# Product-key retrieval with 136 candidate sums of a head in place of 256

## The chip, the cores and the metric

One NeuronCore of a Trainium2 chip runs the whole program; the other cores are idle. The metric is the device time of one execution in microseconds (us), as the median of several executions. All times inside the kernel come from one profiled execution and count from the start of its span.

## What is computed

The program chains eight sublayers over 128 tokens of width 512: four graph layers and four feed-forward layers. The change lies in the fourth, a retrieval by product keys. Of its reference this matters:

```python
q = x @ w_q * (1.0 / np.sqrt(1.0 + BN_EPS))
queries = q.reshape(b, n, 2, HEADS, DIM_KEY).transpose(2, 0, 1, 3, 4)
sim = jnp.einsum('pbnhd,hkpd->pbnhk', queries, keys)
v0, i0 = jax.lax.top_k(sim[0], TOPK)
all_scores = v0[..., :, None] + i0[..., None, :].astype(v0.dtype)
all_scores = all_scores.reshape(*all_scores.shape[:-2], -1)
scores, pk_indices = jax.lax.top_k(all_scores, TOPK)
h = jnp.einsum('bnd,bnhkd->bnhk', q, weights_down)
h = jax.nn.gelu(h)
h = h * jax.nn.softmax(scores, axis=-1)
out = jnp.einsum('bnhk,bnhkd->bnd', h, weights_up)
```

There are 8 heads, 256 keys and a TOPK of 16. The second summand is an index, not a value, so each token and head has 16 best values (sorted, largest first) and their 16 indices; all 16 x 16 sums of a value and an index are formed, the best 16 of these 256 are picked, and their places 0 to 255 name the rows of two tables, `weights_down` and `weights_up`.

A sum of row i (the i-th best value) and the index of rank j among the 16 indices has at least (i + 1)(j + 1) - 1 sums that are no smaller. In rows 8 to 15 an entry whose index is not the largest has at least 17 such sums, so only the entry of the largest index can be among the best 16 there. That leaves 8 x 16 + 8 = 136 candidates.

## The kernel before

All tokens lie on the 128 partitions. Each engine has a queue of its own that is written out by hand in program order; an engine stops at the first wait that isn't met, and waits are on semaphores that other engines (or itself) raise. The retrieval runs from about 104 to 137 us of the span.

**VectorE** runs `search_and_pick(n, n - 2)` (from line 2337) for n = 0 to 9, ten passes. A pass searches head n (n < 8): the 8 largest of its 256 similarities (line 2344), a replacement of these by a very small number (2352), their indices (2357), the next 8 (2359) and their indices (2366). Between these stand the four steps of picking for head p = n - 2 among its 256 sums: the best 8 (2348), their replacement (2355), the next 8 (2362), and a replacement that leaves the rest (2371). At even p from 2 on comes a reciprocal of two heads' weight sums (2375). Head 7's weights are made by VectorE itself (2380), and after the last pass the last reciprocal (2387) and one diagonal (2390).

**ScalarE** (lines 962 to 1002) first computes the GELU (959) and loads the table of the exponential (961). Then for each n in this order: the negated best sum of head n - 2 (964) and the exponentials of its sums (966), the sum of head n - 3's weights (976), the exponentials of head n - 2's rest (971), and the cast of head n's indices to floats (981).

**POOL** (lines 724 to 753) has, for each n: the 256 sums of head n (728, once its cast is done), the weights of head n - 2 (737: exponentials of all sums less those of the rest, so that only the picked keep a weight), and for even n from 4 on two diagonals (745), matrices with the reciprocals of a head's weight sum on the diagonal.

**TensorE** multiplies a head's 128 x 256 weights by its diagonal and adds up the heads (1573), two 128-column halves per head. In between stand parts of later sublayers and spare matmuls against the identity (1220). After the last head the sums are scaled on VectorE (2395) and go through the second table (1581) into the residual.

Four buffers rotate over the heads for the sums, exponentials, rest and weights. The weight matrix of a head always has all 256 columns, since a column stands for a row of the tables.

Of the kernel before, what the change touches and what calls it, by code (L numbers as in the profile page):

```python
# [26 lines left out]
P = 128  # L27
D = 512
CH = D // P
H = 8  # L30
# [19 lines left out]
PICKS = TOPK * TOPK  # L50

# [136 lines left out]
def build(nc, A, out):  # L188
# [14 lines left out]
    with ctx:  # L203
# [112 lines left out]
        best = sb("best", [P, 4, TOPK])  # L316
        negbest = sb("negbest", [P, 4])
# [55 lines left out]
        kv_sb = prob_store[:, :].rearrange("p (b n) -> p b n", b=4)  # L373
        peer_all, peer_exp, peer_rest, peer_pick = (
# [306 lines left out]
        def _(pool):  # L681
# [19 lines left out]
            pool.tensor_scalar(gat_cap[:], ident[:], -2.0 * GAT_NEG, GAT_NEG, ALU.mult, ALU.add).then_inc(sig("gat_loops_ready"), 1)  # L701
# [22 lines left out]
            def head_sums(h):  # L724
                pool.wait_ge(*at("peer_index_ready", h + 1))
                if h:
                    pool.wait_ge(*at("peer_sum_ready", h))
                pool.tensor_tensor(peer_all[:, h % 4, :].rearrange("p (i j) -> p i j", i=TOPK),
                                   topv[:, h % 4, :].unsqueeze(2).broadcast_to([P, TOPK, TOPK]),
                                   topif[:, h % 4, :].unsqueeze(1).broadcast_to([P, TOPK, TOPK]), ALU.add) \  # L730
                    .then_inc(sig("peer_sum_ready"), 1)

            def picked_weights(p):
# [3 lines left out]
                pool.tensor_tensor(peer_pick[:, p % 4, :], peer_exp[:, p % 4, :], peer_rest[:, p % 4, :], ALU.subtract) \  # L737
# [96 lines left out]
        def _(act):  # L834
# [127 lines left out]
            def exp_of_sums(h):  # L962
# [3 lines left out]
                nc.scalar.activation(peer_exp[:, h % 4, :], peer_all[:, h % 4, :], ACT.Exp,  # L966
                                     bias=negbest[:, h % 4:h % 4 + 1]).then_inc(sig("peer_exp_ready"), 1)

            def exp_of_rest(p):
                act.wait_ge(*at("peer_pick_step", PICK_STEPS * (p + 1)))  # L970
                nc.scalar.activation(peer_rest[:, p % 4, :], peer_rest[:, p % 4, :], ACT.Exp,
                                     bias=negbest[:, p % 4:p % 4 + 1]).then_inc(sig("peer_rest_ready"), 1)

            def sum_of_weights(p):
                act.wait_ge(*at("peer_picked", p + 1))
# [1051 lines left out]
        def _(dve):  # L2027
# [130 lines left out]
            dve.wait_ge(*at("gat_loops_ready", 1))  # L2158
# [178 lines left out]
            def search_and_pick(h, p):  # L2337
# [7 lines left out]
                q, work2 = p % 4, peer_work2[:, p % 2, :]  # L2345
                if pick:
                    dve.wait_ge(*at("peer_sum_ready", p + 1))
                    dve.max(best[:, q, 0:8], peer_all[:, q, :]).then_inc(sig("peer_pick_step"), 1)
# [4 lines left out]
                if pick:  # L2353
                    picked(p, 1)
                    dve.match_replace(work2, best[:, q, 0:8], peer_all[:, q, :], NEG).then_inc(sig("peer_pick_step"), 1)
# [11 lines left out]
                if pick:  # L2367
                    picked(p, 3)
                    if p >= 4:
                        dve.wait_ge(*at("peer_picked", p - 3))  # L2370
# [519 lines left out]
```

## Time and profile before

| what | value |
|---|---|
| median of 3 runs | 435.19 us (435.03 to 435.54) |
| the profiled execution | 435.27 us |
| its span, first to last instruction | 433.6 us |
| mean granted TensorE clock | 0.988 of full speed |
| busy in the span: TensorE, VectorE, ScalarE, POOL | 401.1, 197.3, 128.7, 47.2 us |

The profile is of one execution. The page gives busy times, a chain of waits followed back from the last instruction, and the costliest groups of instructions; the timelines give single instructions with their start and listed duration. A listed duration runs from start to end of one instruction, and neighbours on one engine can overlap, so starts and durations say different things. Of two identical instructions the distance of their starts is what the engine spends.

### The profile page before, as it was taken

What the parts mean: (1) busy time and instruction counts of PE and PEld (TensorE: products, weight loads), DVE (VectorE), ACT (ScalarE), POOL (GpSimd) and SP (SyncE); (2) the same over time, 40 slices, a digit from 0 to 9 for tenths busy, and PEclk for the clock granted to TensorE, in tenths of its full rate; (3) what the DMA queues carried; (4) which work ended last, traced back from release to release, by engine and by line L of the source; (5) the groups of instructions that cost most, each with busy time, mean ns of one, the idle gap of its engine ahead of it and who ended that gap; (6) DMA issues with size and microseconds to landing.
All of it is one profiled execution on the core that took longest, in us unless ns stands there. A gap on an engine that the chain in (4) does not pass through costs nothing.

```text
span 433.6 us, 7726 instructions
## 1 busy us (share of the span) xinstructions
PE 401.1 (93%) x2854; PEld 295.0 (68%) x2854; DVE 197.3 (45%) x575; ACT 128.7 (30%) x381; POOL 47.2 (11%) x101
## 2 busy tenths in 40 slices
PE   7998999896588989999999998998999999999996
PEld 6698665796077869997455655665688994493482
DVE  4844545555995244401324558687733531201102
ACT  2313312514453102332300564462113232122130
POOL 4000010010364000011002122011100000000000
PEclk9999999999689999999999999999999999999999
DMA  8999359449002000899998555851920599999900
GB/s 287 383 427 353 122 203 411 163 191 389 3 2 70 29 0 26 310 392 299 374 334 323 182 166 130 303 183 62 400 98 2 226 423 421 421 419 421 384 2 24
DMA packets 19721, 101.44 MB, mean 234 GB/s; under 512 B 3639, under 2 KB 5559, under 8 KB 8804
## 3 DMA queue, kind: packets, MB, share of 16 engines
q1 hardware_dynamic: 19396, 100.94, 61.0%
q8 instruction: 22, 0.36, 0.3%
q14 instruction: 15, 0.12, 0.1%
q10 hardware_dynamic: 288, 0.02, 0.0%
HBM read 100.68 MB, written 0.26 MB: 233 GB/s over the span
## 4 chain that ended last, share of the span: by engine, by line
PE 72%; DVE 12%; issue 7%; ACT 3%; POOL 3%; DVEq 2%; POOLq 0%; ACTq 0%
PE ps L1251 13%; PE ps L1237 12%; PE ps L1636 7%; PE ps L1919 6%; PE ps L1664 4%; PE ps L1220 3%; PE ps L1730 2%; PE ps L1398 2%; PE ps L1653 2%; PE ps L1228 1%; PE ps L1726 1%; PE ps L1985 1%; PE ps L1435 1%; PE ps L1350 1%; PE ps L1271 1%
## 5 line engine op out<-in xcount | busy, mean ns | idle before, releaser
L1220 PE MATMUL ps<-ident 128*128 128x128 f32 x350 | 48.5, 291 | 2.8 <-POOL ident L690 2.8
L1220 PEld LDWEIGHTS ps<-ident 128*128 128x128 f32 x350 | 45.5, 204 | 5.3 <-POOL ident L690 2.8
L1251 PEld LDWEIGHTS ps<-y_t,ew 128*128 128x128 f32 x352 | 39.9, 192 | 1.7 <-issue 1.7
L1251 PE MATMUL ps<-y_t,ew 128*128 128x128 f32 x352 | 40.2, 275 | 0.0
L1636 PE MATMUL ps<-y_t,ew 128*128 128x128 f32 x256 | 29.2, 276 | 0.0
L1636 PEld LDWEIGHTS ps<-y_t,ew 128*128 128x128 f32 x256 | 28.8, 192 | 0.0
L2449 DVE COPY dense<-ps 128x512 f32<-128x512 f32 x8 | 5.5, 692 | 43.7 <-PE ps L1237 43.7
L1237 PE MATMUL ps<-ew,y_t 128*128 128x512 f32 x56 | 25.1, 596 | 0.0
L2731 DVE SCALAR_TENSOR_TENSOR t<-prob_store 128x512 f32<-128x512 f32 x6 | 4.2, 692 | 36.4 <-ACT prob_store L1154 20.4
L867 ACT ACTIVATE prob_store<-ps,nmax_s 128x128 f32<-128x128 f32 x48 | 16.9, 381 | 10.6 <-DVE nmax_s L2111 10.5
L1237 PEld LDWEIGHTS ps<-ew,y_t 128*128 128x128 f32 x56 | 10.2, 190 | 12.0 <-issue 11.8
L1029 ACT ACTIVATE dense<-ps,bqk 128x128 f32<-128x128 f32 x32 | 9.1, 369 | 19.9 <-PE ps L1636 19.9
L855 ACT COPY x<-ps 128x256 f32<-128x256 f32 x10 | 3.7, 372 | 30.3 <-DVE part_st L2075 18.2
L1553 PE MATMUL ps<-dense,eq_t 128*8 128x512 f32 x8 | 5.9, 912 | 7.3 <-ACT big L966 7.3
L1251 PE MATMUL ps<-y_t,dense 128*128 128x128 f32 x96 | 11.2, 277 | 0.7 <-ACT y_t L847 0.7
L1251 PEld LDWEIGHTS ps<-y_t,dense 128*128 128x128 f32 x96 | 10.9, 192 | 1.1 <-issue 1.1
L1237 PE MATMUL ps<-dense,y_t 128*128 128x512 f32 x24 | 11.2, 601 | 0.0
L1237 PE MATMUL ps<-ew,x_t 128*128 128x512 f32 x24 | 11.1, 597 | 0.0
L1884 PE MATMUL ps<-ew,z_t 128*128 128x256 f32 x48 | 10.9, 381 | 0.1
L1664 PE MATMUL ps<-ew,z_t 128*32 128x512 f32 (+1 forms) x56 | 10.9, 597 | 0.0
L705 POOL TENSOR_TENSOR ln_rstd<-ln_mv,minus_half 128x1 f32<-128x1 f32 x8 | 4.6, 570 | 56.6 <-DVE ln_mv L2077 31.2
L774 POOL TENSOR_TENSOR ln_rstd<-ln_mv,minus_half 128x1 f32<-128x1 f32 x10 | 5.5, 545 | 47.9 <-DVE ln_mv L2463 47.9
(545 smaller groups left out, 755.7 us busy)
## 6 DMA issues: line engine op xcount, KB each, us to landing
ew<-in_l_w SPq DMA_DIRECT2D x20, 1024.0 KB, 21.4
dense<-in_l_w SPq DMA_DIRECT2D x12, 1024.0 KB, 20.8
ew<-in_l_wk SPq DMA_DIRECT2D x8, 1024.0 KB, 9.7
ew<-in_l_wq SPq DMA_DIRECT2D x7, 1024.0 KB, 6.1
ew<-in_l_wv SPq DMA_DIRECT2D x6, 1024.0 KB, 8.9
ew<-in_l_wo SPq DMA_DIRECT2D x5, 1024.0 KB, 4.9
ew<-in_gqa_wq SPq DMA_DIRECT2D x3, 1024.0 KB, 10.8
ew<-in_gqa_wk SPq DMA_DIRECT2D x3, 1024.0 KB, 15.4
```

The lines of the kernel that those rows point to most:

```text
L867: last = nc.scalar.activation(prob[:, s, :], ps[:, 3 + a, g * P:(g + 1) * P], ACT.Exp, bias=nmax_s[:, s:s + 1], scale=scale, accum_out=rsu ...
L1029: last = nc.scalar.activation(k_all[:, e, c * P:(c + 1) * P], ps[:, 1 + e % 2, c * P:(c + 1) * P], ACT.Identity, bias=bqk[:, e * 12 + CH + ...
L1220: pe.matmul(ps[:, b, 3 * P:4 * P], ident[:], ident[:], start=True, stop=True)
L1237: return pe.matmul(bank(b), in_t[:, c, :], w[:, c, :], start=(c == 0), stop=(c == CH - 1))
L1251: last = pe.matmul(ps[:, b, m * n:(m + 1) * n], w[:, c, (first + m) * P:(first + m + 1) * P], in_t[:, c, 0:n], start=(c == 0), stop=(c == ...
L1398: last = pe.matmul(ps[:, b, m * P:(m + 1) * P], w[:, m, c, :], y_t[:, c, :], start=(c == 0), stop=(c == CH - 1))
L1636: last = pe.matmul(ps[:, 1 + e % 2, m * P:(m + 1) * P], l2_w("k", e)[:, c, m * P:(m + 1) * P], y_t[:, c, :], start=(c == 0), stop=(c == CH ...
L1653: last = pe.matmul(ps[:, 0, m * P:(m + 1) * P], l2_w("q", p)[:, c, m * P:(m + 1) * P], y_t[:, c, :], start=(c == 0), stop=(c == CH - 1))
L1664: last = pe.matmul(ps[first:end, b, 0:columns.stop - columns.start], in_t[:, c, first:end], l2_w(kind, L2_STEPS[t][a])[:, c, columns], sta ...
L1730: last = pe.matmul(ps[:, b, 0:D // 2], ctx_t[:, c, :], l2_w("o", L2_STEPS[t][0])[:, c, columns], start=(c == 0), stop=(c == CH - 1))
L1884: last = pe.matmul(ps[:, b, 0:D // 2], z_t[:, c, :], l2_w("gcn", k)[:, c, half * D // 2:(half + 1) * D // 2], start=False, stop=(c == CH - 1))
L1919: last = pe.matmul(ps[cols_of, b, :], in_t[:, c, cols_of], w_of[:, c, :], start=(c == 0 and not started), stop=(c == CH - 1))
```

## The change

VectorE takes the largest of a head's 16 indices (`top_index`) and a mark of where it lies (`top_hot`); both stand in the pass after the head's search. POOL forms 8 x 16 sums and 8 further ones, of values 8 to 15 with the largest index. The four picking steps and the two exponentials work on 136 elements. The weights of the 8 late candidates are computed as a column of 8 (`pick_rest`) and spread over 8 x 16 columns by a product with the mark, so that the weight matrix again has 256 columns. Head 7's weights are made in two parts on VectorE, with a drain behind each. POOL's sums now wait for the largest index rather than for the cast, and for no earlier sum. A semaphore used once at the start is replaced by a further step of another.

```diff
@@ -48,6 +48,9 @@
 KEYS = 256
 TOPK = 16
 PICKS = TOPK * TOPK
+ROWS = TOPK // 2
+FULL = ROWS * TOPK
+CANDIDATES = FULL + TOPK - ROWS
 
 SEARCH_STEPS = 5
 PICK_STEPS = 4
@@ -314,6 +317,10 @@
         topi = sb("topi", [P, 4, TOPK], U32)
         topif = sb("topif", [P, 4, TOPK])
         best = sb("best", [P, 4, TOPK])
+        top_index = sb("top_index", [P, 4])
+        top_hot = sb("top_hot", [P, 4, TOPK])
+        pick_rest = sb("pick_rest", [P, 4, TOPK - ROWS])
+        rest_sum = sb("rest_sum", [P, 2])
         negbest = sb("negbest", [P, 4])
         picksum = sb("picksum", [P, H])
         pickinv = sb("pickinv", [P, H])
@@ -371,6 +378,11 @@
         peer_work, peer_work2 = (tile[:, :].rearrange("p (b n) -> p b n", b=2) for tile in (t1, h2))
         wide = big[:, :].rearrange("p (a n) -> p a n", a=2)
         kv_sb = prob_store[:, :].rearrange("p (b n) -> p b n", b=4)
+        def rows_by_top(q, tile, hot):
+            return (tile.rearrange("p (i j) -> p i j", i=ROWS),
+                    pick_rest[:, q, :].unsqueeze(2).broadcast_to([P, TOPK - ROWS, TOPK]),
+                    hot.unsqueeze(1).broadcast_to([P, TOPK - ROWS, TOPK]))
+
         peer_all, peer_exp, peer_rest, peer_pick = (
             tile.rearrange("p (b n) -> p b n", b=4) for tile in (
                 big[:, 0:4 * PICKS], big[:, 4 * PICKS:8 * PICKS], prob_t[:].rearrange("p h n -> p (h n)"),
@@ -698,7 +710,7 @@
                                    fill=1.0, base=0, pattern=[[-1, H], [0, P]], channel_multiplier=1) \
                     .then_inc(sig("gat_r_ready"), 1)
             pool.wait_ge(*at("gat_r_ready", 2))
-            pool.tensor_scalar(gat_cap[:], ident[:], -2.0 * GAT_NEG, GAT_NEG, ALU.mult, ALU.add).then_inc(sig("gat_loops_ready"), 1)
+            pool.tensor_scalar(gat_cap[:], ident[:], -2.0 * GAT_NEG, GAT_NEG, ALU.mult, ALU.add).then_inc(sig("const_ready"), 1)
 
             def layer_norm_rstd(k):
                 pool.wait_ge(*at("ln_var_ready", k + 1))
@@ -722,19 +734,26 @@
             batch_norm_rstd(1)
             layer_norm_rstd(3)
             def head_sums(h):
-                pool.wait_ge(*at("peer_index_ready", h + 1))
-                if h:
-                    pool.wait_ge(*at("peer_sum_ready", h))
-                pool.tensor_tensor(peer_all[:, h % 4, :].rearrange("p (i j) -> p i j", i=TOPK),
-                                   topv[:, h % 4, :].unsqueeze(2).broadcast_to([P, TOPK, TOPK]),
-                                   topif[:, h % 4, :].unsqueeze(1).broadcast_to([P, TOPK, TOPK]), ALU.add) \
+                pool.wait_ge(*at("peer_top_step", 2 * h + 1))
+                pool.tensor_tensor(peer_all[:, h % 4, 0:FULL].rearrange("p (i j) -> p i j", i=ROWS),
+                                   topv[:, h % 4, 0:ROWS].unsqueeze(2).broadcast_to([P, ROWS, TOPK]),
+                                   topif[:, h % 4, :].unsqueeze(1).broadcast_to([P, ROWS, TOPK]), ALU.add) \
+                    .then_inc(sig("peer_sum_ready"), 1)
+                pool.tensor_tensor(peer_all[:, h % 4, FULL:CANDIDATES], topv[:, h % 4, ROWS:TOPK],
+                                   top_index[:, h % 4:h % 4 + 1].broadcast_to([P, TOPK - ROWS]), ALU.add) \
                     .then_inc(sig("peer_sum_ready"), 1)
 
             def picked_weights(p):
                 pool.wait_ge(*at("peer_rest_ready", p + 1))
                 if p >= 4:
                     pool.wait_ge(*at("peer_head_added", p - 3))
-                pool.tensor_tensor(peer_pick[:, p % 4, :], peer_exp[:, p % 4, :], peer_rest[:, p % 4, :], ALU.subtract) \
+                pool.tensor_tensor(pick_rest[:, p % 4, :], peer_exp[:, p % 4, FULL:CANDIDATES],
+                                   peer_rest[:, p % 4, FULL:CANDIDATES], ALU.subtract).then_inc(sig("peer_picked"), 1)
+                pool.tensor_tensor(peer_pick[:, p % 4, 0:FULL], peer_exp[:, p % 4, 0:FULL], peer_rest[:, p % 4, 0:FULL],
+                                   ALU.subtract).then_inc(sig("peer_picked"), 1)
+                pool.wait_ge(*at("peer_picked", 3 * p + 1))
+                pool.wait_ge(*at("peer_top_step", 2 * p + 2))
+                pool.tensor_tensor(*rows_by_top(p % 4, peer_pick[:, p % 4, FULL:], top_hot[:, p % 4, :]), ALU.mult) \
                     .then_inc(sig("peer_picked"), 1)
 
             def diagonals(k):
@@ -963,16 +982,16 @@
                 act.wait_ge(*at("peer_pick_step", PICK_STEPS * h + 1))
                 nc.scalar.mul(negbest[:, h % 4:h % 4 + 1], best[:, h % 4, 0:1], -1.0).then_inc(sig("peer_negbest_ready"), 1)
                 act.wait_ge(*at("peer_negbest_ready", h + 1))
-                nc.scalar.activation(peer_exp[:, h % 4, :], peer_all[:, h % 4, :], ACT.Exp,
+                nc.scalar.activation(peer_exp[:, h % 4, 0:CANDIDATES], peer_all[:, h % 4, 0:CANDIDATES], ACT.Exp,
                                      bias=negbest[:, h % 4:h % 4 + 1]).then_inc(sig("peer_exp_ready"), 1)
 
             def exp_of_rest(p):
                 act.wait_ge(*at("peer_pick_step", PICK_STEPS * (p + 1)))
-                nc.scalar.activation(peer_rest[:, p % 4, :], peer_rest[:, p % 4, :], ACT.Exp,
+                nc.scalar.activation(peer_rest[:, p % 4, 0:CANDIDATES], peer_rest[:, p % 4, 0:CANDIDATES], ACT.Exp,
                                      bias=negbest[:, p % 4:p % 4 + 1]).then_inc(sig("peer_rest_ready"), 1)
 
             def sum_of_weights(p):
-                act.wait_ge(*at("peer_picked", p + 1))
+                act.wait_ge(*at("peer_picked", 3 * (p + 1)))
                 nc.scalar.activation(peer_exp[:, p % 4, :], peer_pick[:, p % 4, :], ACT.Identity,
                                      accum_out=picksum[:, p:p + 1]).then_inc(sig("peer_weights_summed"), 1)
 
@@ -2155,7 +2174,7 @@
                     .then_inc(sig("gat_r_scaled"), 1)
 
             dve.wait_ge(*at("edges_counted", 1))
-            dve.wait_ge(*at("gat_loops_ready", 1))
+            dve.wait_ge(*at("const_ready", 4))
             dve.scalar_tensor_tensor(gat_cap[:], ps[:, 5, 0:P], -2.0 * GAT_NEG, gat_cap[:], ALU.mult, ALU.add) \
                 .then_inc(sig("gat_capped"), 1)
             settle()
@@ -2342,17 +2361,28 @@
                     sim, work = ps[:, 1 + h // 2, w * KEYS:(w + 1) * KEYS], peer_work[:, w, :]
                     dve.wait_ge(*at("peer_sim_ready", h // 2 + 1))
                     dve.max(topv[:, b, 0:8], sim).then_inc(sig("peer_search_step"), 1)
-                q, work2 = p % 4, peer_work2[:, p % 2, :]
+                q, work2 = p % 4, peer_work2[:, p % 2, 0:CANDIDATES]
                 if pick:
-                    dve.wait_ge(*at("peer_sum_ready", p + 1))
-                    dve.max(best[:, q, 0:8], peer_all[:, q, :]).then_inc(sig("peer_pick_step"), 1)
+                    dve.wait_ge(*at("peer_sum_ready", 2 * (p + 1)))
+                    dve.max(best[:, q, 0:8], peer_all[:, q, 0:CANDIDATES]).then_inc(sig("peer_pick_step"), 1)
+                r = h - 1
+                if 0 <= r < H:
+                    dve.wait_ge(*at("peer_index_ready", r + 1))
+                    dve.tensor_reduce(top_index[:, r % 4:r % 4 + 1], topif[:, r % 4, :], AX.X, ALU.max) \
+                        .then_inc(sig("peer_top_step"), 1)
 
                 if search:
                     searched(h, 1)
                     dve.match_replace(work, topv[:, b, 0:8], sim, NEG).then_inc(sig("peer_search_step"), 1)
                 if pick:
                     picked(p, 1)
-                    dve.match_replace(work2, best[:, q, 0:8], peer_all[:, q, :], NEG).then_inc(sig("peer_pick_step"), 1)
+                    dve.match_replace(work2, best[:, q, 0:8], peer_all[:, q, 0:CANDIDATES], NEG).then_inc(sig("peer_pick_step"), 1)
+                if 0 <= r < H:
+                    dve.wait_ge(*at("peer_top_step", 2 * r + 1))
+                    if r >= 4:
+                        dve.wait_ge(*at("peer_picked", 3 * (r - 3)))
+                    dve.tensor_scalar(top_hot[:, r % 4, :], topif[:, r % 4, :], top_index[:, r % 4:r % 4 + 1], None, ALU.is_equal) \
+                        .then_inc(sig("peer_top_step"), 1)
                 if search:
                     dve.max_index(topi[:, b, 0:8], topv[:, b, 0:8], sim).then_inc(sig("peer_search_step"), 1)
                     searched(h, 2)
@@ -2367,8 +2397,8 @@
                 if pick:
                     picked(p, 3)
                     if p >= 4:
-                        dve.wait_ge(*at("peer_picked", p - 3))
-                    dve.match_replace(peer_rest[:, q, :], best[:, q, 8:16], work2, NEG).then_inc(sig("peer_pick_step"), 1)
+                        dve.wait_ge(*at("peer_picked", 3 * (p - 3)))
+                    dve.match_replace(peer_rest[:, q, 0:CANDIDATES], best[:, q, 8:16], work2, NEG).then_inc(sig("peer_pick_step"), 1)
 
                 if p >= 2 and p % 2 == 0:
                     dve.wait_ge(*at("peer_weights_summed", p))
@@ -2377,8 +2407,14 @@
                     picked(p, 4)
                     dve.wait_ge(*at("peer_exp_ready", H))
                     dve.wait_ge(*at("peer_head_added", H - 4))
-                    dve.scalar_tensor_tensor(peer_pick[:, q, :], peer_rest[:, q, :], NEG, peer_exp[:, q, :], ALU.is_equal,
-                                             ALU.mult, accum_out=picksum[:, p:p + 1]).then_inc(sig("peer_pick_step"), 1)
+                    for part, out in ((slice(FULL, CANDIDATES), pick_rest[:, q, :]), (slice(0, FULL), peer_pick[:, q, 0:FULL])):
+                        k = 0 if part.start else 1
+                        dve.scalar_tensor_tensor(out, peer_rest[:, q, part], NEG, peer_exp[:, q, part], ALU.is_equal,
+                                                 ALU.mult, accum_out=rest_sum[:, k:k + 1])
+                        settle()
+                    dve.tensor_tensor(picksum[:, p:p + 1], rest_sum[:, 0:1], rest_sum[:, 1:2], ALU.add)
+                    dve.tensor_tensor(*rows_by_top(q, peer_pick[:, q, FULL:], top_hot[:, q, :]), ALU.mult) \
+                        .then_inc(sig("peer_pick_step"), 1)
 
             for n in range(H + PICK_LAG):
                 search_and_pick(n, n - PICK_LAG)
```

## Rows read from the trace of the kernel before

**Rows 1.** The page's first part: busy time, share of the span and instructions of each engine.

```profile
PE 401.1 (93%) x2854; PEld 295.0 (68%) x2854; DVE 197.3 (45%) x575; ACT 128.7 (30%) x381; POOL 47.2 (11%) x101
```

**Rows 2.** Stretch (us), length, busy (x count) PE, PEld, DVE, ACT, POOL; granted clock, DMA share, GB/s.

```profile
124.00:128.00 4.00, 4.00 (x23) 4.00 (x23) 4.00 (x19) 1.91 (x7) 2.47 (x4) 0.58 0.01 2
128.00:132.00 4.00, 3.44 (x27) 3.15 (x26) 3.07 (x12) 2.95 (x10) 2.25 (x4) 1.00 0.00 0
```

**Rows 3.** The chain of waits, 98 to 150 us: start us, us, what held the chain.

```profile
131.78 0.59 POOL x_t L745
...
132.42 1.29 PE ps L1573 x8
...
140.59 7.38 PE ps L1251 x64
```

**Rows 4.** Timeline of VectorE, one pass: start us, us, engine line operation out<-in.

```profile
114.65 0.42 DVE L2344 MAX8 topv<-ps 128x8 f32<-128x256 f32 x1
114.99 0.41 DVE L2348 MAX8 best<-big 128x8 f32<-128x256 f32 x1
...
117.94 0.15 DVE L2375 RECIPROCAL pickinv<-picksum 128x2 f32<-128x2 f32 x1
```

**Rows 5.** Groups of VectorE by line and shape: busy us, mean ns of one, idle before.

```profile
L2348 DVE MAX8 best<-big 128x8 f32<-128x256 f32 x8 | 3.3, 409 | 0.0
...
L2432 DVE MAX8 gtop<-gate 128x8 f32<-128x8 f32 x2 | 0.3, 170 | 0.1
```

**Rows 6.** Timeline of VectorE, small instructions of a later sublayer.

```profile
170.14 0.23 DVE L2575 TENSOR_SCALAR big<-iota_f,gidxf 128x8 f32<-128x8 f32 x1
170.28 0.23 DVE L2576 TENSOR_SCALAR big<-iota_f,gidxf 128x8 f32<-128x8 f32 x1
...
177.56 0.16 DVE L2558 TENSOR_REDUCE big<-big 128x1 f32<-128x8 f32 x1
177.64 0.15 DVE L2559 TENSOR_REDUCE big<-big 128x1 f32<-128x8 f32 x1
```

**Rows 7.** Timeline of ScalarE at the start of the retrieval.

```profile
106.17 1.28 ACT L961 ACT_TABLE_LOAD   x1
107.47 0.20 ACT L981 CAST topif<-topi 128x16 f32<-128x16 uint32 x1
```

**Rows 8.** Timeline of VectorE, the instruction behind pass 1's first maximum.

```profile
106.33 0.09 DVE L2352 MATCH_VALUE_LOAD t<-topv,ps 128x8 f32 x1
```

**Rows 9.** Timeline of ScalarE, the pass that starts at 114.65 us.

```profile
114.77 0.51 ACT L971 ACTIVATE prob_t<-prob_t,negbest 128x256 f32<-128x256 f32 x1 [0.77 <-DVE prob_t L2371]
115.18 0.19 ACT L981 CAST topif<-topi 128x16 f32<-128x16 uint32 x1
```

**Rows 10.** Groups of ScalarE: an exponential of 128 elements.

```profile
L885 ACT ACTIVATE prob_store<-prob_store,nmax 128x128 f32<-128x128 f32 x8 | 3.1, 390 | 3.1 <-DVE nmax L2170 3.1
```

**Rows 11.** Groups of POOL by line and shape.

```profile
L774 POOL TENSOR_TENSOR ln_rstd<-ln_mv,minus_half 128x1 f32<-128x1 f32 x10 | 5.5, 545 | 47.9 <-DVE ln_mv L2463 47.9
L737 POOL TENSOR_TENSOR prob_store<-big,prob_t 128x256 f32<-128x256 f32 x7 | 5.1, 726 | 1.0 <-ACT prob_t L971 1.0
L728 POOL TENSOR_TENSOR big<-topv,topif 128x256 f32<-128x256 f32 x8 | 4.9, 618 | 21.5 <-ACT topif L981 21.3
...
L770 POOL TENSOR_TENSOR erows<-erows,y 128x512 f32<-128x512 f32 x2 | 2.5, 1270 | 21.8 <-DMA erows<-in_l_rows 21.8
...
L763 POOL MEMSET big<- 128x1 f32 x8 | 0.5, 100 | 0.0
```

**Rows 12.** Timeline of POOL, head 7's sums and head 5's weights.

```profile
128.73 0.62 POOL L728 TENSOR_TENSOR big<-topv,topif 128x256 f32<-128x256 f32 x1 [0.89 <-ACT topif L981]
129.31 0.73 POOL L737 TENSOR_TENSOR prob_store<-big,prob_t 128x256 f32<-128x256 f32 x1
```

**Rows 13.** Timeline of VectorE, head 7's weights and the last reciprocal.

```profile
132.65 0.42 DVE L2380 SCALAR_TENSOR_TENSOR prob_store<-prob_t,big 128x256 f32<-128x256 f32 x1
...
133.12 0.17 DVE L2387 RECIPROCAL pickinv<-picksum 128x2 f32<-128x2 f32 x1
```

## The prediction

> **What bounds the kernel now.** I read four views in this order. The page's first part comes first: TensorE is busy for 93% of the span, VectorE for 45% [rows 1]. An average says little of a stage of 35 us, so the busy time by stretch comes next, over the retrieval: there the reader sees VectorE busy for all 4.00 us of a 4 us stretch, TensorE held up by spare matmuls at a low granted clock, and POOL and ScalarE near half [rows 2]. So between 104 and 128 us VectorE sets the pace. The chain of waits then shows that the last stretch is another one: it leaves VectorE and runs over POOL's diagonal at 131.78 us into the head matmuls at 132.42 us, and from 140.59 us it is TensorE again [rows 3]. What moves those matmuls moves everything after them, one for one: the transfers' share is 0.01 and 0.00 there [rows 2], so no load runs through this end of the stage that could keep its old time. The timelines give the prices.
>
> The profiled execution took 435.27 us (span 433.6 us and 1.67 us around it), 0.08 us over the median of 435.19 us. I add the shift to the median. A measurement of this kernel can tell about 0.2%, 0.87 us, from no change.
>
> I call the ten turns of the VectorE loop passes 0 to 9. Pass n searches head n and picks for head n-2; passes 2 to 7 do both, 8 and 9 only pick.
>
> **The picks, shorter.** Four instructions per head (two maxima, two replacements) fall from 256 to 136 elements. A MAX8 takes 0.409 us on 256 elements and 0.170 on 8 [rows 5], so 0.96 ns an element, and 120 elements fewer save 0.12 us each, 0.48 a head. Instructions without a wait overlap: one MAX8 starts 0.34 us after the one before, though each is listed at 0.41 to 0.42 [rows 4].
>
> **Two small instructions per head, added on VectorE.** The maximum of the 16 indices: the nearest rows are two reductions of 8 elements, 0.08 us from start to start [rows 6]; I take 0.085. The mark (is_equal against a column): two such comparisons start 0.14 us apart [rows 6]; I take 0.145. Together 0.23. So a pass that does both, with no wait, gets 0.48 - 0.23 = 0.25 shorter; six of them: -1.5 us.
>
> Here a rule speaks against the change. By the Trainium skill (VectorE: DVE Perf Modes, The DRAIN you can't avoid) the next instruction cannot issue until the pipe has emptied, so that the count of instructions is what to keep low. By that rule each added instruction would cost its listed time; the starts in the rows show that here it does not. The result it would give is a rival below.
>
> **The wait in pass 1, the largest single term.** The reduction of head 0 stands in pass 1, behind the first maximum of head 1, and waits for ScalarE's cast of head 0's indices. On ScalarE that cast stands behind the loading of the exponential's table, 106.17 to 107.45 us, and ends at 107.47 + 0.20 = 107.67 [rows 7]. Before, only POOL waited for it. VectorE would be at its next instruction at 106.33 us [rows 8]. Now it waits until about 107.71, reduces for 0.085 and goes on at 107.79: +1.46; with the mark 0.145, +1.6 us. Queued behind that wait are all the searches, and nothing covers it, since ScalarE's order is unchanged.
>
> **The same wait in passes 3 to 7.** In the pass that starts at 114.65 us [rows 4], ScalarE's second exponential begins at 114.77, and the cast at 115.18 ends at 115.37 [rows 9], 0.72 into the pass. With 136 elements the exponential falls from 0.51 to about 0.40 (a 128-element one takes 0.390 [rows 10]), so the cast is done at 0.61 and seen at 0.65. VectorE is at the reduction after two maxima, 0.34 + 0.21 = 0.55. The wait is 0.1, and 0.03 in the two passes that come 0.08 later behind a reciprocal: 0.4 in all. Bounds: nothing, if ScalarE is quicker, and 0.2 a pass, if its exponential shrinks by less. Pass 8 then starts at 1.6 - 1.5 + 0.4 = +0.5 us.
>
> **POOL, five instructions where there were two.** Sums of 128, sums of 8, a difference of 8, one of 128, and the spreading product of 128. Nothing shows POOL on two inputs of 8 or 128 elements. Between the listed 0.726 us at 256 elements and 1.270 at 512 [rows 11] lie 2.1 ns an element and 0.18 fixed: 0.45 for a difference of 128, 0.20 for one of 8. The sums, 0.618 at 256 and both inputs spread out, give 0.40 with the same fixed part; the product has their form, 0.40. Bounds for 8 elements: 0.10, a fill of one column, and 0.545, a power of one column, both POOL [rows 11]. For 128 elements: 0.31, half of the sums, and 0.59, a diagonal of 128 columns [rows 3]. I take the two-input line, as nearest in kind. Neighbours overlap by about 0.04 (128.73 to 129.31 us against 0.62 [rows 12]).
>
> **The tail.** From pass 8 on nothing searches, and the path is a relay: ScalarE's exponential of head 5, the cast of head 7, POOL's sums of head 7, its weights of head 5, ScalarE's sum of head 5, its exponential of head 6 (queued behind that sum), POOL's weights of head 6, the diagonal, the matmuls. Changes along it: two exponentials -0.10 each; between cast and sums the reduction steps in, +0.18 (0.16 and two hand-overs, less the one that was); sums 0.36 + 0.16 against 0.58: -0.06; weights 0.16 + 0.41 + 0.40 against 0.71, twice: +0.26 each. Sum +0.44.
>
> VectorE's own end has more to do: the last pass saves 0.48, but head 7's weights, 0.47 us from 132.65 to 133.12 [rows 13], become two masked products with a drain behind each, an addition and a spreading product: about 0.24 + 0.37 + 0.08 + 0.31 = 1.0, +0.53. With the later reciprocal of pass 8 (+0.28) and +0.5 that route ends at +0.8, less than POOL's, so it hides behind it.
>
> At nothing: the renamed semaphore at the start (the same wait, the same event) and the waits for marks of four heads earlier, done a pass before.
>
> **Sum.** +0.5 at pass 8 and +0.44 in the tail: +0.9 us, 435.19 + 0.9 = 436.1 us. By bounds alone: with POOL at its cheap ends (three steps of 8 at -0.1, five of 128 at -0.1) and no waits in passes 3 to 7, POOL's route gives 0.9 - 0.8 - 0.4 = -0.3, and VectorE's, which then sets the end, +0.8 - 0.4 and about 0.4 less for its share of POOL's steps, 0. At POOL's dear ends it is over +3: three steps by 0.34 and five by 0.15 to 0.2, on the path alone, are +1.9, and the loop below adds to it.
>
> **The rivals.** *POOL becomes the bound.* From reduction to reduction there is a loop: POOL's five (1.5), ScalarE's sum (0.5), exponential (0.3), cast (0.2), the reduction and the hand-overs (0.3): 2.8 us. A pass is 3.29 us now (114.65 to 117.94 [rows 4]) and would be 3.1. When POOL's five pass 1.8 us, that loop sets the pass. With the small ones at 0.38, in the middle of their bounds, the pass is 3.2, so some 0.3 over five passes, and the tail gets 0.55 longer: 436.1 + 0.9 = 437.0; at 0.545 it is about 439. For it: fixed costs on POOL are the least known term, and a power of one column costs 0.545. Against: that is a power, and plain differences follow the line. Chance 0.22, around 437.4.
>
> *No change that can be told.* POOL's short instructions lie near the cheap ends and the waits of passes 3 to 7 vanish. The gain of the six passes then pays for pass 1: 435.2 to 435.6. For it: POOL fills a column in 0.10 us. It decides where three short steps cost under 0.4 together. Chance 0.24.
>
> *Faster.* The wait of pass 1 would have to be gone: 436.1 - 1.5 = 434.6. It needs a cast of head 0 before 106.3 us, which the order on ScalarE denies. Chance 0.05.
>
> *Every added instruction costs its listed time.* On VectorE that is 0.16 + 0.23 in place of 0.23, six times: +1.0 on the forecast, 437.1. The overlapping starts speak against it. This is the outcome by the rule named above. Chance 0.05.
>
> *The granted clock.* TensorE's granted clock was 0.58 from 124 to 128 us and 1.00 from 128 to 132 [rows 2]. Were the lower level (1.2 GHz) to hold over the matmuls after 132 us, their 1.29 us for two heads [rows 3] and the like would double: +3, 439. Their order and distances hardly change. Chance 0.03.
>
> **How the numbers follow.** The forecast itself (+0.6 to +1.4) has 0.41. Two thirds of it lie over +0.87, so slower has 0.28 + 0.22 + 0.05 + 0.03 = 0.58; faster 0.05; within 0.2% the rest, 0.37. The range takes in the unmeasurable case down to 435.0 and POOL's middle bounds up to 437.9; outside are the faster case, the dear end of POOL and the clock.
>
> **What would show it.** VectorE idle about 1.4 us near 106.3, released by ScalarE's cast; passes of about 3.1 us; pass 8 starting near 128.4 us; POOL's weights as three rows of about 0.2, 0.45 and 0.40; the matmuls of heads 4 and 5 near 133.3 us; everything after shifted by the same. I am wrong in the mechanism if pass 1 has no such wait, and in size if POOL's 8-element rows are far from 0.2.

## The result, and the profile after

The changed kernel took 437.19 us (median of six executions, 436.42 to 437.22) against 435.26 us for the kernel before on the same chip (six, 435.03 to 435.68): ratio 1.0040, 95% interval 1.0030 to 1.0051 (a ratio is taken over all executions, so it can differ a little from that of the medians). In a second session (e5 below) it took 436.48 against 435.29: 1.0028, 1.0019 to 1.0037. So it is slower, by 1.2 to 1.9 us; the forecast was +0.9, and both results lie inside its range. The profiled execution took 437.22 us, span 435.4. One execution of all that follow, of e6, took 1031.87 us and is left out as a slow run.

The first reading is the page's first part, after:

```profile
PE 403.3 (93%) x2854; PEld 297.2 (68%) x2854; DVE 195.7 (45%) x595; ACT 127.1 (29%) x381; POOL 48.5 (11%) x123
```

Against [rows 1] VectorE has 20 instructions more and is busy 1.6 us less. The shorter picks are there, and the kernel is slower all the same. So the next view is VectorE's timeline, first of the kernel before, at the points that the stage can be measured from (its first search, passes 2 and 8, the first statistics of the residual behind it, and an instruction at 261 us that comes up later):

```profile
103.75 0.43 DVE L2344 MAX8 topv<-ps 128x8 f32<-128x256 f32 x1 [2.42 <-PE ps L1538]
...
108.01 0.41 DVE L2344 MAX8 topv<-ps 128x8 f32<-128x256 f32 x1
...
127.94 0.41 DVE L2348 MAX8 best<-big 128x8 f32<-128x256 f32 x1
...
137.11 0.86 DVE L2075 BATCH_NORM_STATS2 half_st<-ps 128x6 f32<-128x256 f32 x2 [1.46 <-PE ps L1581]
...
261.06 0.88 DVE L2499 SCALAR_TENSOR_TENSOR x<-x,ln_rstd,erows 128x256 f32<-128x256 f32 x2 [0.45 <-issue]
```

The same view of the changed kernel (start us, us, engine, line, operation, output and inputs; in brackets the idle time before it and what ended it):

```profile
103.28 0.43 DVE L2363 MAX8 topv<-ps 128x8 f32<-128x256 f32 x1 [2.42 <-PE ps L1557]
...
107.24 0.17 DVE L2371 TENSOR_REDUCE top_index<-topif 128x1 f32<-128x16 f32 x1 [1.40 <-ACT topif L1000]
107.32 0.08 DVE L2376 MATCH_VALUE_LOAD t<-topv,ps 128x8 f32 x1
...
109.12 0.41 DVE L2363 MAX8 topv<-ps 128x8 f32<-128x256 f32 x1
...
115.27 0.42 DVE L2363 MAX8 topv<-ps 128x8 f32<-128x256 f32 x1
115.61 0.28 DVE L2367 MAX8 best<-big 128x8 f32<-128x136 f32 x1
115.92 0.17 DVE L2371 TENSOR_REDUCE top_index<-topif 128x1 f32<-128x16 f32 x1
116.01 0.08 DVE L2376 MATCH_VALUE_LOAD t<-topv,ps 128x8 f32 x1
...
116.67 0.24 DVE L2384 TENSOR_SCALAR top_hot<-topif,top_index 128x16 f32<-128x16 f32 x1
116.83 0.08 DVE L2387 MATCH_VALUE_LOAD topi<-topv,ps 128x8 f32 x1
...
118.42 0.15 DVE L2405 RECIPROCAL pickinv<-picksum 128x2 f32<-128x2 f32 x1
...
127.88 0.29 DVE L2367 MAX8 best<-big 128x8 f32<-128x136 f32 x1
...
132.38 0.17 DVE L2412 SCALAR_TENSOR_TENSOR pick_rest<-prob_t,big 128x8 f32<-128x8 f32 x1
...
133.41 0.17 DVE L2423 RECIPROCAL pickinv<-picksum 128x2 f32<-128x2 f32 x1
...
137.56 0.86 DVE L2094 BATCH_NORM_STATS2 half_st<-ps 128x6 f32<-128x256 f32 x2 [1.46 <-PE ps L1600]
```

This execution was 0.47 us earlier before anything that the change touches (103.28 against 103.75), so shifts inside the stage are counted from the first search. The whole retrieval, from first search to first statistics, took 137.11 - 103.75 = 33.36 us before and 137.56 - 103.28 = 34.28 after: **+0.92**, against +0.94 by the steps of the prediction (0.5 and 0.44).

The loss is in pass 1. Its reduction waits 1.40 us for ScalarE, whose cast stands behind the table load in the changed kernel as it did in [rows 7]:

```profile
105.71 1.28 ACT L980 ACT_TABLE_LOAD   x1
107.00 0.20 ACT L1000 CAST topif<-topi 128x16 f32<-128x16 uint32 x1
```

The next instruction, a value load, started at 106.33 us before [rows 8] and at 107.32 here: +0.99, and with the 0.47 of the earlier start +1.46. POOL's five instructions by groups, over the stretch 103 to 136 us (count, busy us and mean ns, then idle time before):

```profile
L738 POOL TENSOR_TENSOR big<-topv,topif 128x128 f32<-128x128 f32 x8 | 3.2, 401 | 21.1 <-DVE top_index L2371 21.1
L752 POOL TENSOR_TENSOR prob_store<-big,prob_t 128x128 f32<-128x128 f32 x7 | 3.2, 455 | 0.0
L756 POOL TENSOR_TENSOR prob_store<-pick_rest,top_hot 128x128 f32<-128x128 f32 x7 | 2.8, 400 | 0.0
L742 POOL TENSOR_TENSOR big<-topv,top_index 128x8 f32<-128x8 f32 x8 | 1.6, 202 | 0.0
L750 POOL TENSOR_TENSOR pick_rest<-big,prob_t 128x8 f32<-128x8 f32 x7 | 1.4, 203 | 0.9 <-ACT prob_t L990 0.9
```

They take 1.66 us in all where two took 1.34 [rows 11]. Up to pass 7 they wait for VectorE's reduction and are not what VectorE waits for. In the tail they are on the path, and POOL's timeline has the diagonal that the matmuls of heads 4 and 5 wait for:

```profile
132.16 1.24 POOL L764 TENSOR_SCALAR x_t<-ident,pickinv 128x128 f32<-128x128 f32 x2
```

**The rest of the first result.** The span grew by 1.8 us (433.6 to 435.4), though the retrieval grew by 0.92 and began 0.47 early. The shift of like instructions along VectorE's timeline is +0.45 at the end of the retrieval and again from 204 to 260 us; it is +0.08 behind the 0.45 us idle at 261.06 us above, which the changed kernel does not have there, and +0.43 at 293.7 us, where it has one. Then, between 295 and 297 us, it jumps to +1.15, and to +1.57 by 311 us. The busy time by stretch shows why (stretch, length, TensorE busy and count, granted clock, DMA share, GB/s):

```profile
295.00:296.00 1.00, 0.83 (x4) 1.00 0.00 0
296.00:297.00 1.00, 0.87 (x10) 0.67 0.00 0
297.00:298.00 1.00, 1.00 (x17) 0.50 0.00 0
298.00:299.00 1.00, 0.94 (x16) 0.50 0.00 0
299.00:300.00 1.00, 1.00 (x3) 0.63 0.00 0
```

TensorE's granted clock fell to the lower level, 1.2 GHz, for some 3 us; in the profile of before it is 1.00 over the same stretch. That cost +1.14 us (+0.43 to +1.57). TensorE had stood idle for 1.56 us ahead of 295.1 us (1.22 before), waiting for VectorE; e5's profile has the same 1.56 us of idle and no fall, so the idle alone does not bring it.

The last 0.31 us lies at the program's end, behind the issue of the output's write, before:

```profile
431.11 0.36 SPq L676 DMA_DIRECT2D out_x<-acc  x1
```

and after:

```profile
432.69 0.35 SPq L688 DMA_DIRECT2D out_x<-acc  x1
```

From there to the last instruction the trace has 2.44 us before and 2.75 after. The write lands 2.0 us after its issue in both; what is longer is the distance of POOL's last two semaphore steps, 0.08 us before and 0.40 after. All seven profiles of kernels with 136 sums show this, none of the five with 256, so it comes with the changed program, whatever the order of the retrieval. The parts add up: 0.92 of retrieval, less 0.47 of start, 1.14 of clock and 0.31 at the end are 1.90 us, and the span grew by 1.89 in the trace. This is one execution; e5 takes another.

### The profile page after: what moved, and what is told of

It reads as the page before. It is cut to its first block, busy times and chain, and to the rows that moved or that the text cites. A ratio compares the mean times of both kernels' runs of the same rounds, so it can differ in the third digit from the quotient of the medians.

```text
span 435.4 us, 7774 instructions
## 1 busy us (share of the span) xinstructions
PE 403.3 (93%) x2854; PEld 297.2 (68%) x2854; DVE 195.7 (45%) x595; ACT 127.1 (29%) x381; POOL 48.5 (11%) x123
## 4 chain that ended last, share of the span: by engine, by line
PE 74%; DVE 11%; issue 6%; ACT 4%; POOL 3%; DVEq 2%; POOLq 0%; ACTq 0%
PE ps L1270 13%; PE ps L1256 12%; PE ps L1655 7%; PE ps L1938 6%; PE ps L1683 4%; PE ps L1239 4%; PE ps L1749 2%; PE ps L1417 2%; PE ps L1672 2%; PE ps L1592 1%; PE ps L1300 1%; PE ps L1745 1%; PE ps L1247 1%; PE ps L2004 1%; PE ps L1454 1%
```

## The experiments

The account by the terms says: the pass-1 wait costs 1.4 to 1.5 us, six shorter passes give back 1.2, the longer relay adds 0.4 and the program's end 0.3. Its rivals, as the expectations letter them, put the loss elsewhere. Each run goes beside the kernel before on the same chip.

**e1, the cast ahead of the table load.** The wait of pass 1 is taken out of the changed kernel: ScalarE loads the exponential's table behind head 0's cast.

```diff
-            act.preload_act_table(ACT.Exp)
...
                     indices(n)
+                if n == 0:
+                    act.preload_act_table(ACT.Exp)
```

> The changed kernel, with ScalarE's cast of head 0's indices ahead of its load of the exponential's table (nothing else moved). Theory A (VectorE's wait in pass 1 is the largest loss): the reduction of head 0 starts about 0.1 us after the first maximum of pass 1 in place of 1.4 us after it, so the retrieval ends about 1.3 us earlier: its last matmuls 0.4 us earlier than in the kernel before. The time falls by 1.3 us to about 435.9 us, and to about 434.9 if the low granted clock near 296 us goes too. Rival B (POOL's five instructions and the relay of the tail are the loss): the earlier passes only wait more at the end, the gain is under 0.4 us. Rival C (the later part of the program loses time by itself, whatever the shift): the retrieval gains 1.3 us and the low clock near 296 us stays.

Measured: 435.13 us (twelve executions) against 435.33, ratio 0.9999 (0.9988 to 1.0011). VectorE's timeline:

```profile
103.35 0.43 DVE L2364 MAX8 topv<-ps 128x8 f32<-128x256 f32 x1 [2.42 <-PE ps L1558]
...
136.20 0.86 DVE L2095 BATCH_NORM_STATS2 half_st<-ps 128x6 f32<-128x256 f32 x2 [1.46 <-PE ps L1601]
```

and ScalarE's:

```profile
105.65 0.20 ACT L999 CAST topif<-topi 128x16 f32<-128x16 uint32 x1
105.87 1.28 ACT L1012 ACT_TABLE_LOAD   x1
```

The retrieval takes 32.85 us: 1.43 less than the changed kernel, 0.51 less than before. So the wait is more than the whole loss of the retrieval, and rival B falls; the load of 1.28 us still runs, where nothing waits for it. In time the 0.51 us less the 0.31 at the program's end leave 0.20, and by that the medians differ; the interval takes in no change at all.

**e2, the wait alone, added to the kernel before.** No work changes; VectorE only waits in pass 1.

```diff
+                if h == 1:
+                    dve.wait_ge(*at("peer_index_ready", 1))
                 if search:
```

> The kernel before, with one wait added and nothing else: in pass 1 VectorE waits for ScalarE's cast of head 0 behind its first maximum. Theory A: 1.35 to 1.4 us of idle VectorE near 106.3 us, every pass later by as much, and nothing takes it up: the first matmuls of heads 4 and 5 at about 133.8 us in place of 132.4, the time 436.6 us. Rival B: the tail's relay has slack, so the time is under 0.5 us longer. Rival C (a shift of this stage brings more than itself behind it): over 437 us, with a low granted clock near 296 us in the profile.

Measured: 436.55 us (eleven) against 435.33, ratio 1.0021 (1.0012 to 1.0030). VectorE's timeline:

```profile
107.71 0.09 DVE L2354 MATCH_VALUE_LOAD t<-topv,ps 128x8 f32 x1 [1.40 <-ACT topif L981]
...
138.41 0.86 DVE L2075 BATCH_NORM_STATS2 half_st<-ps 128x6 f32<-128x256 f32 x2 [1.46 <-PE ps L1581]
```

The same 1.40 us of idle, and a retrieval of 34.65 us (first search at 103.76): +1.29. The wait alone, without any of the new arithmetic, makes the kernel before as slow as the changed one is in e5.

**e4, POOL's weights ahead of its sums,** on top of e1. In the tail POOL's sums of head 7 run ahead of head 5's weights, though those are what TensorE waits for.

```diff
             for n in range(H + 1):
-                if n < H:
-                    head_sums(n)
                 if n >= PICK_LAG:
                     picked_weights(n - PICK_LAG)
+                if n < H:
+                    head_sums(n)
```

> As the kernel with the early cast, and POOL makes the weights of head n-2 ahead of the sums of head n. In the tail, head 5's weights then need not stand behind the sums of head 7, nor these behind the reduction. Theory A with the relay of the prediction: head 5's weights start about 0.8 us earlier, so the reciprocal in pass 8, head 6's weights and the matmuls of heads 4 and 5 come 0.6 to 0.8 us earlier than with the early cast alone: about 435.2 us, or 434.2 if the low clock near 296 us goes too. Rival B': VectorE's own route (four picks and head 7's two-part weights) is as long as POOL's, and the gain is under 0.3 us.

Measured: 434.62 us (twelve) against 435.33, ratio 0.9980 (0.9970 to 0.9991). POOL's timeline, head 5's first difference and then head 7's sums:

```profile
126.99 0.21 POOL L750 TENSOR_TENSOR pick_rest<-big,prob_t 128x8 f32<-128x8 f32 x1 [0.46 <-ACT prob_t L989]
...
127.93 0.40 POOL L738 TENSOR_TENSOR big<-topv,topif 128x128 f32<-128x128 f32 x1
```

The sums follow the weights, and the retrieval takes 31.93 us: -1.43 against before and -0.92 against e1, so rival B' falls.

**e5, the changed kernel again,** unaltered, to see whether the granted clock's fall belongs to it.

> The changed kernel once more, unaltered, with a profile of its own and more executions. What is open: its profile showed the retrieval ending 0.92 us later against its start, and 1 us more behind it, of which a low granted clock near 296 us is the largest part. Theory A (the clock there differs from execution to execution): the executions lie in groups about 1 us apart, near 436.2 and 437.2 us, and a profile without the low clock near 296 us is 0.9 to 1.2 us over the kernel before. Theory C (it belongs to the changed kernel): all executions near 437.2 us, the low clock there again.

Measured: 436.48 us (eleven, 436.13 to 437.26) against 435.29, ratio 1.0028 (1.0019 to 1.0037). Its chain of waits at the end of the retrieval:

```profile
132.20 0.40 POOL prob_store L756
132.60 0.60 POOL x_t L764
133.25 1.33 PE ps L1592 x8
```

The retrieval is 34.25 us, +0.89; the matmuls of heads 4 and 5 start at 133.25 us, +0.83 on [rows 3], or +0.86 from the first search, which was 0.03 us earlier. The granted clock stayed at 1.00 from 284 to 304 us, and the span grew by 1.1 us: the retrieval and the 0.31 us at the end. So the fall is not a fixed part of the change. Of the 17 executions of the changed kernel over both sessions ten lie between 436.1 and 436.8 us and seven between 437.06 and 437.26. That the seven are those with a fall is shown for one alone: the mean granted clock, the only sign of the clock that executions without a profile left, does not part the groups (0.976 to 0.988 in the seven, 0.983 to 0.988 in the ten).

**e6, spare matmuls against the fall,** in the idle stretch ahead of 296 us.

```diff
             probs_t(4)
+            keep_clock(2, times=4)
             x1_transposes(3)
```

> The changed kernel with four more spare transposes-sized matmuls on TensorE (into an unused quarter bank) at the stop near 293.5 us where it waited 1.56 us for VectorE; nothing in the retrieval differs. Theory A: the retrieval shows the same times, the granted clock near 296 us stays at the upper level in the profile, and the time is 436.2 us, 0.9 us over the kernel before, in nearly all executions. Theory C' (the later loss is not the clock's): 437.2 us as before.

Measured: 436.33 us (nine) against 435.29, ratio 1.0026 (1.0017 to 1.0036). The profile shows 1.00 from 284 to 303 us, but so does that of e5, and the median is within 0.2 us of e5's. Slower executions still came, up to 437.45. Inconclusive on how many of them the fall accounts for.

**e7, a plain delay at the end of the retrieval,** in the kernel before: two fills on VectorE with a wait behind each, ahead of head 7's weights. It asks what a delay of about 1 us there costs at the end of the kernel. (e3, a first form of it without the waits, gave no time.)

```diff
                     dve.wait_ge(*at("peer_head_added", H - 4))
+                    for _ in range(2):
+                        dve.memset(h2[:], 0.0)
+                        settle()
```

> The kernel before, with two fills of a 512-column tile on VectorE, each with a drain, between the last pick and head 7's weights: about 1.1 us of delay, of which 0.2 to 0.3 lies beside POOL's route, so that the retrieval ends 0.8 to 0.9 us later with no other change of its order, the shift that the changed kernel has there. Theory A: 436.2 us, with some executions 1 us above where the clock near 296 us falls. Rival C (a shift of this size always costs twice): near 437.2 us.

Measured: 436.47 us (eleven) against 435.29, ratio 1.0020 (1.0011 to 1.0029). The retrieval grew by 1.04 us, the median by 1.18. A later end of the retrieval is paid once here, not twice, and rival C falls.

**e8, POOL's order of e4 in the kernel before,** with 256 sums and the old place of the table load.

> The kernel before with POOL's weights of head n-2 ahead of the sums of head n, all else as it was. It tells how much of the gain of the reordered 136-sum kernel (434.62 us) is POOL's order alone. Theory A: in the tail head 5's weights no longer stand behind head 7's sums, so the reciprocal of pass 8 comes 0.6 to 0.7 us earlier and the end by 0.5 to 0.6: 434.7 to 434.8 us, so that 136 sums with the early cast are worth no more than 0.2 us over 256. Rival D: VectorE, full through pass 7 with 256-element picks, then sets the end by its own four picks of pass 9, the gain is under 0.3 us and 136 sums are worth 0.5 us or more.

Measured: 434.64 us (eleven) against 435.29, ratio 0.9985 (0.9976 to 0.9994); the retrieval is 32.78 us, -0.58. The order alone, without the change, is worth about what e4 is in the median, and rival D falls. POOL's timeline of the tail, to be held against [rows 12], where the sums stand first:

```profile
128.16 0.73 POOL L737 TENSOR_TENSOR prob_store<-big,prob_t 128x256 f32<-128x256 f32 x1 [0.88 <-ACT prob_t L971]
128.85 0.62 POOL L728 TENSOR_TENSOR big<-topv,topif 128x256 f32<-128x256 f32 x1
```

**e9 and e10, both reordered kernels side by side** (e4's and e8's, unaltered), and **e11, e4 with e6's spare matmuls,** all on one chip.

> The 136-sum kernel with the early cast and POOL's weights ahead of its sums, unaltered, beside the 256-sum kernel with the same order of POOL on one chip. Their profiles had the retrieval's end 0.8 us apart, their medians, from two chips, 0.02. Theory A (the medians hide 0.4 to 0.8 us behind the clock of single executions): 0.4 us or more under the reordered 256-sum kernel on the same chip. Rival E (136 sums are worth nothing on the time): within 0.2 us of it.

> The kernel before with POOL's weights ahead of its sums, once more, as the other half of the comparison: 434.6 us by both theories.

> As the reordered 136-sum kernel, with four spare matmuls at TensorE's stop near 291 us, where the changed kernel's first profile had the clock fall. Theory A (part of the executions loses about 1 us there): the slow group of executions thins out, the median is 434.2 us. If the slow executions lose their time elsewhere: no change against the reordered 136-sum kernel.

Measured, against 435.55 us for before: e9 434.93 (ratio 0.9985, 0.9976 to 0.9994), e10 435.06 (0.9989, 0.9980 to 0.9998), e11 434.50 (0.9972, 0.9961 to 0.9983). The retrievals took 32.78, 32.78 and 31.93 us. The two reordered kernels lie 0.13 us apart on one chip, so theory A falls and rival E holds: with this order of POOL, 136 sums are worth nothing on the time that these runs can tell. Of the 0.85 us by which e4's and e11's retrievals are shorter than e10's, the program's end takes back 0.31. e9 is e4's kernel, and in its execution the retrieval itself was no shorter; where its 0.85 us went is seen in the busy time by stretch (columns as in [rows 2]):

```profile
124.00:128.00 4.00, 4.00 (x20) 4.00 (x20) 3.64 (x21) 2.25 (x10) 3.52 (x10) 0.50 0.01 2
```

and in that of e11:

```profile
124.00:128.00 4.00, 2.99 (x24) 2.69 (x23) 3.64 (x22) 2.49 (x11) 3.29 (x10) 1.00 0.01 2
```

In e9 TensorE ran at 1.2 GHz there, and its spare matmuls lasted to 131.79 us, 1.2 us after POOL's diagonal was ready (about 130.6); in e11's execution the clock stood at 1.00. The spell at the lower clock differs between executions of one kernel: e4's profile has 0.78 over this stretch where e9's has 0.50. **e11 has the lowest median against its own chip's kernel before**, 1.05 us under it, where the changed kernel is 1.2 to 1.9 over; its interval overlaps those of e4 and e8. Its slowest execution (434.73 us) lies under e9's slower ones (up to 435.41), as its theory A has it, but with seven executions. Its spare matmuls stand behind 290 us, so the higher clock at 124 us is not their work, and why its median is 0.43 us under e9's is not shown.

**Where e4's and e8's gain goes.** In their profiles, which also start 0.44 and 0.48 us early, both keep it to 315 us, and lose 0.4 us of it between there and 318 us. In e8, TensorE's timeline:

```profile
310.68 1.10 PE L1862 MATMUL ps<-qk_t,first_row 128*128 128x256 f32 x4 [0.36 <-DMA v<-in_gcn_b]
```

TensorE waits 0.36 us for a load, and its spare transposes run behind that; VectorE's scale for the matmuls after them is there 1.09 us earlier than in before's profile, and they start 0.56 us earlier. e11's profile shows the same wait with 0.30 us; before's has none. e10, the same kernel as e8, loses only 0.06 us there in its execution, so this too differs between executions, and what sets the load's landing was not followed.

## Why the prediction was right, step by step

The forecast was 436.1 us, +0.9, and the mechanism held at each step up to the end of the retrieval, where +0.92 and +0.89 were measured. The time came out at +1.2 to +1.9. What the sum lacked are 0.31 us at the program's end, a term that the prediction put at nothing without a word, and in the first result 1.14 us of a lower clock. e5's +0.89 and the 0.31 make +1.20, and its medians differ by 1.19. That the first result fell inside the range too is luck: the range reached to 437.9 for POOL's prices, which were not what made it slower.

- **The pass-1 wait.** +1.46 was forecast for VectorE's next instruction, +1.46 measured; e1 and e2 show from both sides that this one wait, and not the new arithmetic, makes the retrieval slower.
- **Shorter picks.** A maximum of 136 elements takes 0.28 us against 0.41 [rows 4]; -0.12 was forecast, -0.13 measured.
- **Two small instructions.** From start to start the reduction holds VectorE for 0.09 us (115.92 to 116.01; forecast 0.085) and the mark for 0.16 (116.67 to 116.83; 0.145). A pass is 118.42 - 115.27 = 3.15 us against 3.29. The rival that each added instruction costs its listed time falls: the rows list 0.17 and 0.24 us. By the Trainium skill (VectorE: DVE Perf Modes, The DRAIN you can't avoid) the next instruction would start only when the pipe has emptied, except one that is not held; this trace agrees with the exception, not with the rule (MAX8 on 136 elements: 0.28 us listed, the next instruction 0.20 us after its start).
- **Passes 3 to 7, and pass 8.** The reduction would have been free to start 0.20 us behind the maximum, at 115.81 us, and started at 115.92: a wait of 0.1, as forecast. From the first search of pass 2 to the start of pass 8 VectorE takes 127.88 - 109.12 = 18.76 us against 127.94 - 108.01 = 19.93: the six passes give back 1.17 us, and 1.1 was forecast (1.5 less 0.4 of waits). Pass 8 starts at 127.88 against 127.94, +0.41 after taking off the 0.47 of the start; +0.5 was forecast.
- **POOL.** 0.40, 0.20, 0.20, 0.455 and 0.40 us were measured; 0.40, 0.20, 0.20, 0.45 and 0.40 forecast. The line through two lengths of a two-input operation held down to 8 elements, so the rival of POOL as the bound, which wanted 0.38 there, falls, and so does that of no change, which wanted POOL cheaper.
- **The tail.** From the start of pass 8 to the diagonal that the matmuls of heads 4 and 5 wait for, the relay takes 132.16 - 127.88 = 4.28 us against 131.78 - 127.94 = 3.84 [rows 3]: +0.44, and +0.44 was forecast. VectorE's own end: head 7's weights took 133.41 - 132.38 = 1.03 us (1.0 forecast, 0.47 before [rows 13]), and the last reciprocal came 0.29 + 0.47 = 0.76 us later (0.8 forecast), hidden behind POOL's route as said.
- **"Everything after shifted by the same."** This is the step that did not hold as the prediction put it. In e5 the shift is +0.86 us after the retrieval, +0.48 behind 261 us and +0.82 behind 293 us, so it is kept but for an idle that moved; then the program's end adds its 0.31. In the first result the granted clock added 1.14. And that no load could keep its old time was read from the transfers at the retrieval's end alone: a load at 310 us took 0.4 us from the gain of e4 and e8. The rival of the granted clock was priced over the matmuls after 132 us and given a chance of 0.03; the clock struck at 296 us, which the prediction had not looked at.

What stays open: how large a part of the 437 us executions the fall explains, what makes POOL's last step 0.31 us later, and what sets apart e9 and e11. (e1's profile is 0.57 us under before's, 434.70 against 435.27, and its median 0.20; 0.40 of the profile's gain is an earlier start.)

## What to carry to other kernels

A wait on another engine that is put into an in-order loop is to be priced at the first turn too, where the producer may stand behind something that happens once, such as a table load: here 1.4 us at one place outweighed the 1.2 us of six shortened passes. When a stage ends in a relay over four engines, the order of a helper engine's two jobs can be worth more than shortening them (e8: -0.58 us for moving two lines). And what a stage gains is worth only what the rest of the program leaves of it: a load or a spell at the lower clock behind it, and here 0.31 us at the program's end, where the changed kernel is slower though nothing there was edited.

## What the runs showed of the hardware that was not expected

**An idle of VectorE that moves with the program.** The 0.45 us at 261.06 us before has no releaser. In the changed kernel it is gone there, and stands at another instruction:

```profile
293.72 0.75 DVE L2531 SCALAR_TENSOR_TENSOR x<-t,ln_mv,erows 128x512 f32<-128x512 f32 x1 [0.45 <-issue]
```

All profiles of kernels with 136 sums have it at the second place; of those with 256, e8 and e10 have it at the first as before has, e7 two instructions earlier (260.61 us), and e2 shows none there. Some 0.65 us behind it the DMA view shows, in each kernel, one packet of an instruction queue; before, over 261.5 to 262 us (packets, MB, share):

```profile
q14 instruction: 1, 0.01, 6.6%
```

and after, over 294.2 to 294.7 us:

```profile
q14 instruction: 1, 0.01, 6.2%
```

The other kernel has no such packet from 259.5 to 262 and from 293.3 to 295.3 us. It looks as if VectorE stood still at the border of a block of its program, and 20 instructions more shift which instruction that is; no run tested it, and e2, which has a packet at 262 us without such an idle ahead of it, does not speak for it. By the Trainium skill (Runtime: NRT & Kernel Launch, Instruction fetch mechanics) an engine fetches its program in blocks and the cost of crossing a border is mostly hidden; if it is this, 0.45 us of it shows here.

**POOL's end, later by 0.31 us.** The 0.40 us between POOL's last two semaphore steps, against 0.08 with 256 sums, may be of the same kind: in all seven profiles with 136 sums, and in none of the other five, the same queue has a packet 0.7 to 1.0 us behind the later step. In the first result's profile, over 435.5 to 436.5 us:

```profile
q14 instruction: 1, 0.01, 2.8%
```

This was not tested either.

**The start differs between executions.** The first search lies at 103.75 us in before's profile and 103.28 in the changed kernel's, but at 103.72 in e5 and 103.42 in e10: the 0.47 us is there at 8 us already, and goes with the execution, not with the kernel.
